# A mixture-of-experts layer: the second product on plain f32 operands instead of f32r high and low parts

## The chip, the core and the metric

The kernel runs on one core of a Trainium2 chip. The core has a matrix engine (TensorE, PE; its weight loads are shown apart as PEld), a vector engine (VectorE, DVE), an activation engine (ScalarE, ACT), a general engine (GpSimd, POOL) and a sync engine (SyncE, SP) that mostly issues transfers. The engines run their own programs and meet at semaphores. The metric is the device time of one execution in microseconds; lower is better.

## The reference, cut to what matters

Three stages follow each other on 32 sequences of 128 tokens with 128 features: the gradient of a soft sequence alignment, an attention with 8 heads, and a layer of 8 experts of which each token uses two. The change is in the last:

```python
def _L0_ffn_ref(x, Wg, W, V, W2):            # x: (32, 128, 128), layer-normed
    gate_logits = jnp.einsum('bsd,de->bse', x, Wg)
    topv, topi = jax.lax.top_k(gate_logits, K)          # K = 2 of E = 8
    w = jax.nn.softmax(topv, axis=-1)
    gw = jnp.sum(w[..., None] * jax.nn.one_hot(topi, E, dtype=x.dtype), axis=-2)
    y = jnp.zeros_like(x)
    for e in range(n_experts):                          # W, V: (8, 128, 512), W2: (8, 512, 128)
        h = jax.nn.silu(jnp.einsum('bsd,df->bsf', x, W[e])) * jnp.einsum('bsd,df->bsf', x, V[e])
        y = y + gw[..., e:e + 1] * jnp.einsum('bsf,fd->bsd', h, W2[e])
    return y
```

All of it is f32. `h @ W2[e]` is the second product.

## The kernel before

**Alignment** (0 to about 230 us) is a wavefront on DVE, ACT and POOL. **Attention** (about 230 to 590 us) works in 32 steps n, one block of 128 tokens each, with pieces that serve four blocks at once. The order on each engine is written out by hand: one Python loop over `STEPS_OF_ATTENTION` per engine, in which `pair` and `quad` place each piece some steps ahead or behind. Its last pieces sort every token's two copies by expert into the DRAM buffer `xd_dram` (POOL, L1038).

In the same steps the weights of the experts are brought in, in 24 chunks, chunk c in step c: SP loads 128x512 floats into one of two `stage` tiles (`load_weights`, L480 to L489), ACT copies them to an f32r tile as the high part (`weights_high`, L927 to L930), and DVE subtracts it from the f32 value for the low part (`weights_low`, L1405 to L1408). Chunks 0 to 15 are W and V, chunks 16 to 23 are W2, whose parts lie side by side in `wdn`.

**Experts** (about 590 to 820 us) works through 72 tiles of 128 token copies, all of one expert each. A product of two f32 matrices is done on f32r operands as high x high + high x low + low x high. For tile k:

- SP loads the rows (L517); PE turns them (`column`, L707); ACT copies the high part (`columns`, L953), DVE makes the low part (`column_low`, L1467).
- PE computes both first products, three matmuls of 512 columns each (`up`, L541 to L543, within the helper `three`).
- ACT applies silu (L959), DVE multiplies (`hidden`, L1453).
- PE turns the result in four pieces (`turn`, L727); ACT copies the high part to `xnt_hi` (`hidden_high`, L965), DVE makes the low part `xnt_lo` (`hidden_low`, L1474).
- PE computes the second product (`down`, L743 to L747): for each of four pieces, high part times both parts of `wdn` (256 columns, L743 and L747) and low part times the high one (128 columns, L744 and L746). Columns 0 to 127 of bank 6 then hold two of the three sums, columns 128 to 255 the third.
- ACT scales the third by the token's gate (`gated_low`, L973), DVE scales the others and adds it (`gated`, L1482), and POOL scatters the rows to `y_dram` (L1064).

The stages of different tiles are interleaved: on PE `up(k)`, `column(k + 1)`, `turn(k - 1)`, `down(k - 2)`. The expert of a tile is read from a table in `tili` by PE itself (`expert_of`, L756). PE's loop turns every eight tiles (`pe.Fori`, L780), DVE's and ACT's every four. `down(k)` waits for `s_y` of the tile before, since there is one bank 6; `up(k)` waits for `column_low(k)`.

At the end (820 to 844 us) SP loads the scattered rows, DVE adds them and SP stores the output.

Of the kernel before, what the change touches and what calls it, by code (L numbers as in the profile page):

```python
# [5 lines left out]
def tower(nc, tok_x, tok_y, we_t, w_proj, b_proj, w_gap, b_gap, iota66, wqk_pl, wv_bd, w_m, w_g, w_up, v_up, w_down,  # L6
# [27 lines left out]
    with ctx:  # L34
# [36 lines left out]
        nvt = sb("nvt", [128, NB])  # L71
        thf = sb("thf", [T, NB, T])
# [55 lines left out]
        ones_f = al("ones_f", [128, 128])  # L128
# [8 lines left out]
        zdiag = al("zdiag", [128, NB])  # L137
# [5 lines left out]
        wdn = sb("wdn", [128, NX, FC, 2, E], fr)  # L143

        def parts_of(c):

            kind, e = c // NX, c % NX
            staged = stage[c % 2][:]
            if kind == 2:
                return wdn[:, e, :, 0, :], wdn[:, e, :, 1, :], staged.rearrange("p (c n) -> p c n", n=E)  # L150
            hi, lo = ((wup_hi, wup_lo), (vup_hi, vup_lo))[kind]
            return hi[:, e, :], lo[:, e, :], staged
# [61 lines left out]
        hidt_hi, hidt_lo = xnt_hi, xnt_lo  # L214
        dest = sb("dest", [128, 4], i32)
        ylow = [on[1][:, k, :] for k in range(2)]
# [45 lines left out]
        s_wlo = sem("s_wlo")  # L262
        s_wraw = sem("s_wraw")
# [3 lines left out]
        s_htl = sem("s_htl")  # L267
# [55 lines left out]
        s_ylow = sem("s_ylow")  # L323
# [94 lines left out]
        CHUNKS = 3 * NX  # L418
# [3 lines left out]
        def _(sp):  # L422
# [57 lines left out]
            def load_weights(c):  # L480
# [4 lines left out]
                if kind < 2:  # L485
                    sp.dma_start(stage[c % 2][:], (w_up, v_up)[kind][e]).then_inc(s_stage[c % 2], 16)
                else:
                    sp.dma_start(stage[c % 2][:].rearrange("p (c n) -> p c n", n=E),
                                 w_down[e].rearrange("(c p) n -> p c n", p=128)).then_inc(s_stage[c % 2], 16)  # L489
# [48 lines left out]
        def _(pe):  # L538
# [181 lines left out]
            def turn(k, c):  # L720

                pe.wait_ge(s_hid, k + 1)
                if not (isinstance(k, int) and k < 2):
                    pe.wait_ge(s_ht, k - 1)
                    pe.wait_ge(s_htl, k - 1)
# [5 lines left out]
            def down(k, c, e):  # L731

                pe.wait_ge(s_ht, k + 1)
                pe.wait_ge(s_htl, k + 1)
                if not (isinstance(k, int) and k < 1):
                    pe.wait_ge(s_y, k)
                for n in range(FC):
                    b = slice(T * n, T * n + T)

                    low = [hidt_lo[c % 2][:, b], wdn[:, bass.ds(e, 1), n, 0, :].rearrange("p e n -> p (e n)")]  # L740
                    both = wdn[:, bass.ds(e, 1), n, :, :].rearrange("p e j n -> p (e j n)")
                    if n == 0:
                        nc.tensor.matmul(ps[:, 6, 0:2 * E], hidt_hi[c % 2][:, b], both, start=True, stop=False)  # L743
                        nc.tensor.matmul(ps[:, 6, 0:E], *low, start=False, stop=False)  # L744
                    else:
# [6 lines left out]
            pe.wait_ge(s_wlo, CHUNKS)  # L752
            pe.wait_ge(s_table, 1)
# [31 lines left out]
        def _(act):  # L785
# [175 lines left out]
            def hidden_high(k, c):  # L961
# [3 lines left out]
                nc.scalar.activation(hidt_hi[c % 2][:], ps[:, 5 + 2 * (c % 2), :], ACT.Copy).then_inc(s_ht, 1)  # L965

            def gated_low(k, c):

                act.wait_ge(s_dn, k + 1)
                act.wait_ge(s_dest, k + 1)  # L970
                if not (isinstance(k, int) and k < 2):
                    act.wait_ge(s_y, k - 1)
                nc.scalar.activation(ylow[c % 2], ps[:, 6, E:2 * E], ACT.Copy,  # L973
                                     scale=rowgate[:, c:c + 1]).then_inc(s_ylow, 1)

            def act_tile(k, c, head=False, tail=0):
# [4 lines left out]
                if not (head and k < 1) and tail < 3:  # L981
                    hidden_high(k - 1, (c + 3) % 4)
                if not (head and k < 2):
# [585 lines left out]
```

## Time and profile before

| | |
|---|---|
| median of 3 runs | 842.27 us (841.99 to 842.51) |
| profiled execution | 846.1 us |
| its span | 844.0 us |
| PE busy | 484.8 us (57%), weight loads 422.3 |
| DVE busy | 593.4 us (70%) |
| ACT busy | 406.8 us (48%) |
| POOL busy | 230.7 us (27%) |
| mean granted clock of PE | 0.983 |

The profile is one execution. Busy time is the time in which an engine's instructions run; matmuls overlap each other, so PE can read as busy while it could take more. A matmul's record covers its passage through the array, so the pace is read from the distance between starts, not from the durations. Shapes of f32r operands are printed without numbers or as f32.

### The profile page before, as it was taken

To read this page: it belongs to the slowest core of one execution; us is meant where nothing else is said; L and a number is where in the kernel's file an instruction comes from. 1 tells how busy PE (TensorE), PEld (TensorE's weight loads), DVE (VectorE), ACT (ScalarE), POOL (GpSimd) and SP (SyncE) were. 2 spreads that over 40 slices of the span, in tenths; PEclk is the share of its full clock that TensorE was granted. 3 is DMA by queue.
4 is the path that set the end of the run, shared out by engine and by line. 5 is a ranking of instruction groups with operands and counts; after the bars stand their busy time and mean duration, and the time that the engine had idled before them with its cause. 6 is when DMAs were issued, how large, how long until landed. Compare 5 with 4: busy or idle time off the path is not lost.

```text
span 844.0 us, 13480 instructions
## 1 busy us (share of the span) xinstructions
PE 484.8 (57%) x2622; PEld 422.3 (50%) x2623; DVE 593.4 (70%) x2029; ACT 406.8 (48%) x1180; POOL 230.7 (27%) x417
## 2 busy tenths in 40 slices
PE   1200000000004689899899998620899999999960
PEld 0200000000003578798788987610688888888850
DVE  3698989889747866978988674652466666666645
ACT  1344444444302867666666574100566656666630
POOL 1054545455300000000403312455133333333330
PEclk9999999999999999999999999999999999999985
DMA  4499230403254122222102000012111111111109
GB/s 98 90 177 165 45 72 10 82 1 81 41 137 125 51 75 63 63 75 62 52 26 67 26 7 20 26 38 64 35 45 42 44 43 44 41 43 43 44 16 287
DMA packets 113385, 54.18 MB, mean 64 GB/s; under 512 B 56652, under 2 KB 109132, under 8 KB 113251
## 3 DMA queue, kind: packets, MB, share of 16 engines
q1 hardware_dynamic: 106366, 44.60, 22.7%
q0 software_dynamic: 4352, 8.47, 3.0%
q10 hardware_dynamic: 2621, 0.62, 0.5%
q8 instruction: 14, 0.23, 0.1%
q14 instruction: 32, 0.26, 0.1%
HBM read 29.93 MB, written 24.26 MB: 64 GB/s over the span
## 4 chain that ended last, share of the span: by engine, by line
PE 36%; DVE 31%; issue 20%; DMA 5%; SPq 4%; ACT 3%; ACTq 0%; DVEq 0%; POOLq 0%
DVE D L1178 5%; PE ps L541 5%; DVE D L1153 5%; PE ps L543 5%; PE ps L542 5%; PE ps L747 4%; PE ps L627 4%; PE ps L727 4%; PE ps L632 3%; ACT D L819 2%; DVE D L1144 2%; PE ps L746 2%; PE ps L743 2%; DVE rc L1322 2%; DVE ps L1133 1%
## 5 line engine op out<-in xcount | busy, mean ns | idle before, releaser
L1038 POOL DMA_INDIRECT xd_dram<-pay,slot x64 | 64.8, 1013 | 281.3 <-DVE pay L1402 263.9
L632 PEld LDWEIGHTS ps<-va,pt 128*128 128x128 f32 x512 | 137.5, 351 | 0.0
L627 PE MATMUL ps<-eye_sb,sq 128*128 128x128 f32 x256 | 114.8, 454 | 13.9 <-DVE on L1339 10.3
L1064 POOL DMA_INDIRECT y_dram<-on,dest x72 | 70.7, 982 | 164.1 <-DVE on L1482 127.5
L632 PE MATMUL ps<-va,pt 128*128 128x17 f32 x512 | 114.7, 307 | 0.0
L577 PE MATMUL ps<-zdiag,ones_f 32*128 32x32 f32 x2 | 0.6, 406 | 193.0 <-DVE zdiag L1221 193.0
L627 PEld LDWEIGHTS ps<-eye_sb,sq 128*128 128x128 f32 x256 | 87.5, 343 | 34.4 <-issue 25.8
L577 PEld LDWEIGHTS ps<-zdiag,ones_f 32*128 32x128 f32 x2 | 0.5, 304 | 193.1 <-DVE zdiag L1221 193.1
L1022 POOL TENSOR_TENSOR D<-D 128x128 f32<-128x128 f32 x130 | 56.3, 433 | 129.3 <-DVE D L1171 65.0
L1453 DVE TENSOR_TENSOR sq<-sq,ps 128x512 f32<-128x512 f32 x72 | 49.5, 688 | 56.2 <-PE ps L543 41.1
L819 ACT ACTIVATE D<-D 64x2 f32<-64x2 f32 (+1 forms) x154 | 31.4, 204 | 106.9 <-DVE D L1153 86.9
L898 ACT ACTIVATE sq<-sq,mn 128x128 f32<-128x128 f32 x256 | 78.0, 395 | 0.0
L747 PE MATMUL ps<-wdn,xnt_hi 128*128 x216 | 57.8, 336 | 0.0
L959 ACT ACTIVATE sq<-ps 128x512 f32<-128x512 f32 x72 | 43.1, 598 | 27.1 <-PE ps L543 27.1
L891 ACT ACTIVATE sq<-ps 128x1024 f32<-128x1024 f32 x32 | 32.7, 1022 | 46.4 <-DVE mn L1324 42.2
L1178 DVE TENSOR_TENSOR_SCAN D<-ps,D 128x64 f32<-128x64 f32 x130 | 45.5, 350 | 13.5 <-ACT D L819 0.5
L1322 DVE TENSOR_REDUCE rc<-ps 128x8 f32<-128x1024 f32 x32 | 39.0, 1218 | 22.7 <-PE ps L607 11.9
L1474 DVE TENSOR_TENSOR xnt_lo<-ps,xnt_hi 128x512 fp32r<-128x512 f32 x72 | 49.8, 692 | 6.7 <-ACT xnt_hi L965 0.7
L746 PE MATMUL ps<-wdn,xnt_lo 128*128 x216 | 52.1, 241 | 0.0
L1153 DVE TENSOR_TENSOR_SCAN D<-ps,D 128x64 f32<-128x64 f32 x130 | 44.8, 345 | 6.9 <-DMA D<-th_dram 4.8
L965 ACT ACTIVATE xnt_hi<-ps 128x512 fp32r<-128x512 f32 x72 | 43.1, 598 | 7.6 <-PE ps L727 1.5
L607 PE MATMUL ps<-kx,qs 32*128 32x512 f32 x64 | 38.8, 705 | 11.0 <-ACT sq L891 7.5
(226 smaller groups left out, 1474.1 us busy)
## 6 DMA issues: line engine op xcount, KB each, us to landing
stage<-xd_dram SPq DMA_DIRECT2D x72, 65.0 KB, 1.8
D<-th_dram SPq DMA_DIRECT2D x16, 208.0 KB, 4.8
g_dram<-D SPq DMA_DIRECT2D x14, 208.0 KB, 4.6
x_dram<-D SPq DMA_DIRECT2D x14, 208.0 KB, 4.7
h0q<-g_dram SPq DMA_DIRECT2D x8, 256.0 KB, 3.0
gb<-g_dram SPq DMA_DIRECT2D x8, 256.0 KB, 3.5
xf<-x_dram SPq DMA_DIRECT2D x8, 256.0 KB, 3.2
xb<-x_dram SPq DMA_DIRECT2D x8, 256.0 KB, 3.5
```

Of the source, the lines that this page charges most:

```text
L627: last = nc.tensor.transpose(ps[:, 5 + h // 4, T * (h % 4):T * (h % 4) + T], sq[n % 3][:, T * h:T * h + T], eye_sb[:])
L632: m = nc.tensor.matmul(ps[:, 7, (HD + 1) * h:(HD + 1) * (h + 1)], pt[turned % 2][:, T * h:T * h + T], va[q % 2][:, k, h, :], start=True, s ...
L746: nc.tensor.matmul(ps[:, 6, 0:E], *low, start=False, stop=False)
L747: m = nc.tensor.matmul(ps[:, 6, 0:2 * E], hidt_hi[c % 2][:, b], both, start=False, stop=(n == FC - 1))
L898: m = nc.scalar.activation(v, v, ACT.Exp, bias=mn[:, n % 3, h:h + 1], scale=-1.0 / HD ** 0.5)
L1022: pool.tensor_tensor(C3[:, k, 0:2, :], shifted(M, at, 1, 2), bass.AP(tensor=n.tensor, offset=n.offset, ap=[n.ap[0], [H, 1], [0, 2], [1, H] ...
L1038: pool.indirect_dma_start(xd_dram, bass.IndirectOffsetOnAxis(slot[:, q, j, k:k + 1], 0), pay[q % 2][:, k, j, :], None).then_inc(s_sc[2 * k ...
L1064: pool.indirect_dma_start(y_dram, bass.IndirectOffsetOnAxis(dest[:, c:c + 1], 0), yrow[c], None, bounds_check=2 * NB * T - 1, oob_is_err=F ...
L1153: nc.vector.tensor_tensor_scan(row(M, at), above(k), TH[:, s, :], cells(M, at, 0, 1), ALU.max, ALU.subtract).then_inc(s_row, 1)
L1178: nc.vector.tensor_tensor_scan(row(X, at), weights_of(i * ROWS + k)[:, 2, :], V[:, k % 2, :], cells(X, at, 0, 1), ALU.mult, ALU.add).then_ ...
L1322: link(V_.tensor_reduce(rc[:, 0, :], ps[:, 3:5, :].rearrange("p a (h s) -> p (a h) s", s=T), AX.X, ALU.min, apply_absolute_value=True))
L1474: V_.tensor_tensor(hidt_lo[c % 2][:], ps[:, 5 + 2 * (c % 2), :], hidt_hi[c % 2][:].bitcast(f32), ALU.subtract).then_inc(s_htl, 1)
```

## The change

The weights W2 are loaded straight to their place, unsplit, in the same steps of the attention stage. The turned hidden tile is copied once, to new f32 tiles `hidt` (two, 128x512), and the second product is four f32 matmuls of 128 columns. `hidden_low` and `gated_low` are gone, and `gated` reads only bank 6. `zdiag` and `ones_f` move from the space that the alignment shares with later tiles to space of their own.

```diff
-        wdn = sb("wdn", [128, NX, FC, 2, E], fr)
+        wdn = sb("wdn", [128, NX, FC, E])
...
-        hidt_hi, hidt_lo = xnt_hi, xnt_lo
+        hidt = [sb(f"hidt{k}", [128, 512]) for k in range(2)]
...
-        CHUNKS = 3 * NX
+        CHUNKS = 2 * NX
...
+            def load_down(e):
+
+                sp.dma_start(wdn[:, e, :, :], w_down[e].rearrange("(c p) n -> p c n", p=128)).then_inc(s_wd, 16)
...
                 if 0 <= n + 3 < CHUNKS:
                     load_weights(n + 3)
+                if CHUNKS <= n < CHUNKS + NX:
+                    load_down(n - CHUNKS)
...
             def down(k, c, e):
 
                 pe.wait_ge(s_ht, k + 1)
-                pe.wait_ge(s_htl, k + 1)
                 if not (isinstance(k, int) and k < 1):
                     pe.wait_ge(s_y, k)
                 for n in range(FC):
-                    b = slice(T * n, T * n + T)
-
-                    low = [hidt_lo[c % 2][:, b], wdn[:, bass.ds(e, 1), n, 0, :].rearrange("p e n -> p (e n)")]
-                    both = wdn[:, bass.ds(e, 1), n, :, :].rearrange("p e j n -> p (e j n)")
-                    if n == 0:
-                        nc.tensor.matmul(ps[:, 6, 0:2 * E], hidt_hi[c % 2][:, b], both, start=True, stop=False)
-                        nc.tensor.matmul(ps[:, 6, 0:E], *low, start=False, stop=False)
-                    else:
-                        nc.tensor.matmul(ps[:, 6, 0:E], *low, start=False, stop=False)
-                        m = nc.tensor.matmul(ps[:, 6, 0:2 * E], hidt_hi[c % 2][:, b], both, start=False,
-                                             stop=(n == FC - 1))
+                    m = nc.tensor.matmul(ps[:, 6, 0:E], hidt[c % 2][:, T * n:T * n + T],
+                                         wdn[:, bass.ds(e, 1), n, :].rearrange("p e n -> p (e n)"),
+                                         start=(n == 0), stop=(n == FC - 1))
                 m.then_inc(s_dn, 1)
 
             pe.wait_ge(s_whi, CHUNKS)
             pe.wait_ge(s_wlo, CHUNKS)
+            pe.wait_ge(s_wd, 16 * NX)
...
-            def gated_low(k, c):
...
-                nc.scalar.activation(ylow[c % 2], ps[:, 6, E:2 * E], ACT.Copy,
-                                     scale=rowgate[:, c:c + 1]).then_inc(s_ylow, 1)
...
-            def hidden_low(k, c):
-                dve.wait_ge(s_ht, k + 1)
-                if not (isinstance(k, int) and k < 2):
-                    dve.wait_ge(s_dn, k - 1)
-                V_.tensor_tensor(hidt_lo[c % 2][:], ps[:, 5 + 2 * (c % 2), :], hidt_hi[c % 2][:].bitcast(f32),
-                                 ALU.subtract).then_inc(s_htl, 1)
...
             def gated(k, c):
 
-                dve.wait_ge(s_ylow, k + 1)
+                dve.wait_ge(s_dn, k + 1)
...
-                V_.scalar_tensor_tensor(yrow[c], ps[:, 6, 0:E], rowgate[:, c:c + 1], ylow[c % 2], ALU.mult,
-                                        ALU.add).then_inc(s_y, 1)
+                V_.tensor_scalar(yrow[c], ps[:, 6, 0:E], rowgate[:, c:c + 1], None, ALU.mult).then_inc(s_y, 1)
```

PE, inside the loop over the tiles, from the last turned pieces of one tile to its second product. Before (`sq` holds the hidden tile, `xnt_hi` and `xnt_lo` its turned parts; ISA rows compute an address from the expert's number):

```order
L727 MATMUL ps<-eye_sb,sq 128x128 x3
L756 ISA
L756 TENSOR_LOAD tili
L756 ISA x2
L743 ISA [waits s_y,s_htl,s_ht]
L743 MATMUL ps<-wdn,xnt_hi 128x256
L744 MATMUL ps<-wdn,xnt_lo 128x128
L746 ISA
L746 MATMUL ps<-wdn,xnt_lo 128x128
L747 MATMUL ps<-wdn,xnt_hi 128x256
```

PE at the same place now (L724 is the turning, L745 the table, L734 the second product):

```order
L724 MATMUL ps<-eye_sb,sq 128x128 x3
L745 ISA
L745 TENSOR_LOAD tili
L745 ISA x2
L734 ISA [waits s_y,s_ht]
L734 MATMUL ps<-wdn,hidt 128x128
L734 ISA
L734 MATMUL ps<-wdn,hidt 128x128
```

The product keeps its place behind the turning and the table read, and keeps its wait for `s_y`; the wait for the low part is gone.

DVE, one tile inside its loop, before:

```order
L1453 TENSOR_TENSOR sq<-sq,ps 128x512 [waits s_htp,s_up]
L1464 REGISTER_ALU
L1466 ISA [waits s_xc]
L1467 TENSOR_TENSOR ont_lo<-ps,ont_hi 128x128 [waits s_up]
L1460 COPY rowgate<-stage 128x1 [waits s_ys3,s_xr3]
L1461 CAST dest<-stage 128x1
L1474 TENSOR_TENSOR xnt_lo<-ps,xnt_hi 128x512 [waits s_dn,s_ht]
L1482 SCALAR_TENSOR_TENSOR on<-ps,rowgate,on 128x128 [waits s_ys1,s_ylow]
```

DVE now (L1431 was L1453, L1445 was L1467, L1453 was L1482):

```order
L1431 TENSOR_TENSOR sq<-sq,ps 128x512 [waits s_htp,s_up]
L1442 REGISTER_ALU
L1444 ISA [waits s_xc]
L1445 TENSOR_TENSOR ont_lo<-ps,ont_hi 128x128 [waits s_up]
L1438 COPY rowgate<-stage 128x1 [waits s_ys2,s_xr2]
L1439 CAST dest<-stage 128x1
L1453 TENSOR_SCALAR on<-ps,rowgate 128x128 [waits s_ys0,s_dn]
```

The subtraction is gone, and the last operation waits for PE (`s_dn`) where it waited for ACT (`s_ylow`).

## Rows read from the trace of the kernel before

**Rows 1.** The page, 40 slices of the span: PE busy tenths and granted clock.
```profile
PE   1200000000004689899899998620899999999960
...
PEclk9999999999999999999999999999999999999985
```

**Rows 2.** Stretches: from:to, length, busy us (count) by engine, clock, DMA share, GB/s.
```profile
400.00:475.00 75.00, 70.40 (x330) 62.34 (x330) 61.83 (x220) 48.06 (x125) 19.19 (x18) 1.00 0.15 46
...
700.00:800.00 100.00, 97.73 (x629) 84.97 (x628) 67.70 (x199) 60.75 (x132) 32.41 (x33) 1.00 0.16 43
```

**Rows 3.** Groups, 600 to 800 us: line, shapes, count | busy, mean ns | idle before.
```profile
L747 PE MATMUL ps<-wdn,xnt_hi 128*128 x198 | 52.4, 333 | 0.0
...
L1474 DVE TENSOR_TENSOR xnt_lo<-ps,xnt_hi 128x512 fp32r<-128x512 f32 x67 | 46.3, 692 | 5.9 <-ACT xnt_hi L965 0.2
...
L973 ACT ACTIVATE on<-ps,rowgate 128x128 f32<-128x128 f32 x65 | 23.9, 367 | 31.5 <-PE ps L747 30.2 <-DVE dest L1461 1.3
```

**Rows 4.** One tile on PE in time order: start us, us, engine, line, operation.
```profile
623.98 0.42 PE L541 MATMUL ps<-wup_hi,ont_hi 128*128 x1
...
625.50 0.60 PE L727 MATMUL ps<-eye_sb,sq 128*128 128x128 f32 x4
...
626.87 0.40 PE L541 MATMUL ps<-wup_hi,ont_hi 128*128 x1
```

**Rows 5.** All engines in time order at the loop's turn.
```profile
626.70 0.33 PE L747 MATMUL ps<-wdn,xnt_hi 128*128 x1
...
627.54 0.35 DVE L1482 SCALAR_TENSOR_TENSOR on<-ps,rowgate,on 128x128 f32<-128x128 f32 x1
...
628.80 0.19 PEld L744 LDWEIGHTS ps<-wdn,xnt_lo 128*128 128x128 f32 x1
...
629.16 0.28 DVE L1467 TENSOR_TENSOR ont_lo<-ps,ont_hi 128x128 fp32r<-128x128 f32 x1
...
629.49 0.19 PEld L747 LDWEIGHTS ps<-wdn,xnt_hi 128*128 128x128 f32 x1
...
630.14 0.19 PEld L541 LDWEIGHTS ps<-wup_hi,ont_hi 128*128 128x128 f32 x1 [0.46 <-issue]
...
632.77 0.19 PEld L743 LDWEIGHTS ps<-wdn,xnt_hi 128*128 128x128 f32 x1 [0.62 <-issue]
```

**Rows 6.** PE in time order, the first tile of the experts.
```profile
593.50 0.63 PE L542 MATMUL ps<-wup_lo,ont_hi 128*128 x1
593.93 0.63 PE L543 MATMUL ps<-wup_hi,ont_lo 128*128 x1
```

**Rows 7.** Plain f32 products in time order.
```profile
34.23 0.50 PEld L571 LDWEIGHTS ps<-raw_m,raw_v 128*128 128x128 f32 x2 [9.24 <-DVE cnt L1109]
34.23 0.80 PE L571 MATMUL ps<-raw_m,raw_v 128*128 128x128 f32 x2 [8.97 <-DVE cnt L1109]
...
34.95 0.58 PE L572 MATMUL ps<-uv,cnt 22*128 22x1 f32 x2
...
412.78 1.85 PE L673 MATMUL ps<-wg_sb,x3t 128*128 128x8 f32 x8 [2.38 <-issue]
```

**Rows 8.** The last tile's second product in time order.
```profile
814.88 0.58 PE L743 MATMUL ps<-wdn,xnt_hi 128*128 x1 [1.04 <-DVE on L1482]
...
815.58 0.52 PE L747 MATMUL ps<-wdn,xnt_hi 128*128 x1
...
816.43 0.52 PE L747 MATMUL ps<-wdn,xnt_hi 128*128 x1
```

**Rows 9.** Instructions on wdn (ns min/median/max, from, to), then PE's waits, 400 to 475 us.
```profile
L1408 DVE TENSOR_TENSOR wdn<-stage,wdn x8: 679/682/685, 415.2 to 472.4; 128x512 fp32r<-128x512 f32 x8
...
PE ps L673 <- issue: 3.7, 2, 2.4
```

**Rows 10.** DVE and PE in time order, one step of the attention stage.
```profile
442.53 0.68 DVE L1408 TENSOR_TENSOR wdn<-stage,wdn 128x512 fp32r<-128x512 f32 x1
...
446.81 0.57 PE L673 MATMUL ps<-wg_sb,x3t 128*128 128x8 f32 x2 [1.28 <-issue]
```

More of the change, by code:

```diff
@@ L71, in tower @@
         nvt = sb("nvt", [128, NB])
+        zdiag = sb("zdiag", [128, NB])
+        ones_f = sb("ones_f", [128, 128])
         thf = sb("thf", [T, NB, T])
@@ L213, in tower @@
         hid = [sq[1][:, F * k:F * k + F] for k in range(2)]
-        hidt_hi, hidt_lo = xnt_hi, xnt_lo
+        hidt = [sb(f"hidt{k}", [128, 512]) for k in range(2)]
         dest = sb("dest", [128, 4], i32)
-        ylow = [on[1][:, k, :] for k in range(2)]
         rowgate = sb("rowgate", [128, 4])
@@ L262, in tower @@
         s_wlo = sem("s_wlo")
+        s_wd = sem("s_wd")
         s_wraw = sem("s_wraw")
@@ L484, in load_weights @@
                 need(sp, s_wlo, c - 1)
-                if kind < 2:
-                    sp.dma_start(stage[c % 2][:], (w_up, v_up)[kind][e]).then_inc(s_stage[c % 2], 16)
-                else:
-                    sp.dma_start(stage[c % 2][:].rearrange("p (c n) -> p c n", n=E),
-                                 w_down[e].rearrange("(c p) n -> p c n", p=128)).then_inc(s_stage[c % 2], 16)
+                sp.dma_start(stage[c % 2][:], (w_up, v_up)[kind][e]).then_inc(s_stage[c % 2], 16)
+            def load_down(e):
+                sp.dma_start(wdn[:, e, :, :], w_down[e].rearrange("(c p) n -> p c n", p=128)).then_inc(s_wd, 16)
             for n in STEPS_OF_ATTENTION:
@@ L959, in silu, with hidden_turned @@
                 nc.scalar.activation(act_up[c % 2], ps[:, 1 + c % 2, :], ACT.Silu).then_inc(s_silu, 1)
[L961 removed]
+            def hidden_turned(k, c):
                 act.wait_ge(s_htp, k + 1)
@@ L964, in hidden_high @@
                     act.wait_ge(s_dn, k - 1)
-                nc.scalar.activation(hidt_hi[c % 2][:], ps[:, 5 + 2 * (c % 2), :], ACT.Copy).then_inc(s_ht, 1)
-            def gated_low(k, c):
-                act.wait_ge(s_dn, k + 1)
-                act.wait_ge(s_dest, k + 1)
-                if not (isinstance(k, int) and k < 2):
-                    act.wait_ge(s_y, k - 1)
-                nc.scalar.activation(ylow[c % 2], ps[:, 6, E:2 * E], ACT.Copy,
-                                     scale=rowgate[:, c:c + 1]).then_inc(s_ylow, 1)
+                nc.scalar.activation(hidt[c % 2][:], ps[:, 5 + 2 * (c % 2), :], ACT.Copy).then_inc(s_ht, 1)
             def act_tile(k, c, head=False, tail=0):
@@ L981, in act_tile @@
                 if not (head and k < 1) and tail < 3:
-                    hidden_high(k - 1, (c + 3) % 4)
-                if not (head and k < 2):
-                    gated_low(k - 2, (c + 2) % 4)
+                    hidden_turned(k - 1, (c + 3) % 4)
             columns(0, 0)
@@ L991, in _ @@
                     act_tile(t + c, c)
-            for k in range(TILES - 4, TILES + 2):
+            for k in range(TILES - 4, TILES + 1):
                 act_tile(k, k % 4, tail=max(0, k - TILES + 2))
@@ L1491, in dve_tile @@
                     destination(k, c)
-                if not (head and k < 1) and tail < 3:
-                    hidden_low(k - 1, (c + 3) % 4)
                 if not (head and k < 2):
```

9 lines of the change are left out of this document (removed).

## The prediction

> **What bounds the kernel now.** I read the page first: PE is full from slice 14 on, in the attention stage and then, from about 590 us, in the experts [rows 1]. The change touches the experts, and the conversion of their weights, which sits in the attention stage. The stretches come next [rows 2]: between 700 and 800 us PE is busy for 97.7 of 100 us, DVE for 67.7 and ACT for 60.8. So PE sets the pace of a tile, and work taken from DVE or ACT there gives nothing by itself. In the groups L747 runs 198 times in 200 us, three per tile, hence 66 tiles of 3.03 us [rows 3].
>
> Then I read one tile in order of time [rows 4]. From L541 at 623.98 to the next tile's L541 at 626.87 are 2.89 us: six products of 512 columns and a turned tile up to 625.50, then four turned pieces of 128 f32 columns, (0.60 - 0.27)/3 = 0.11 apart (0.60 is the group, 0.27 the passage of one), and the second product. With 0.11 for the turned tile the six are (625.50 - 623.98 - 0.11)/6 = 0.235 apart. What limits the second product's eight matmuls is their weight loads, not their columns: from the second load (628.80) to the eighth (629.49) are six steps in 0.69 us, 0.115 each [rows 5], with matmuls of 128 and 256 columns behind them in turn.
>
> The difference between 3.03 and 2.89 is time in which PE has nothing issued: at the loop's turn, which comes every eight tiles, the first load of L541 (630.14) has 0.46 us of "issue" before it, and the first load of L743 after it (632.77) has 0.62 [rows 5].
>
> PE's clock: the six products of the very first tile are 0.43 apart (593.50 to 593.93) [rows 6], later ones 0.235 [rows 4]. These are the two levels, 1.2 and 2.4 GHz. The page's clock line reads 9 in the attention stage too [rows 1], but L673 there has eight loads (1.85 - 0.36)/7 = 0.21 apart [rows 7], and 0.21 is also the pace of loads in the last tile, (816.43 - 815.58)/4, where the page's line shows the lower level [rows 1, 8]. I go by the spacings: attention ran at 1.2 GHz.
>
> **Part 1: the second product on PE.** Four plain f32 matmuls of 128 columns per tile take the place of eight f32r ones. The trace records every plain f32 product twice: L571 is one matmul in the code and has two loads and two matmuls, L673 is four and has eight [rows 7]; turned f32 pieces are recorded once, four for four [rows 4]. So there are again eight passes per tile, each with a weight load of 128 f32 columns. What one pass costs is the disputed number; the trace has no f32 product of 128 columns at the higher clock. Its loads: L673's take 0.21 at 1.2 GHz as the f32r ones do [rows 7, 8], so at 2.4 GHz they cost the same 0.115. Its columns: L571 is the one case, at 1.2 GHz (it runs at 34 us, among PE's first work). Its second load starts at 34.23 + 0.50 - 0.34 = 34.39 (0.34 is one load's passage) and its second matmul at 34.23 + 0.80 - 0.42 = 34.61: the first pass of columns took at most 0.22, or 0.11 at 2.4 GHz. The second ended before L572 begins at 34.95, at most 0.34, or 0.17 [rows 7]. Four turned pieces of 128 f32 columns go 0.11 apart at the higher clock [rows 4]. So the ends for a pass are 0.11 and 0.17, and I take 0.115, the value next to the turned pieces: load and columns run beside each other, and the load is the longer by a hair. 8 x 0.115 = 0.92 per tile before and after: **0 us**. At 0.17 it would be 0.055 x 8 x 72 = +32 us. At the other end little is to be had: L541 also waits for DVE's L1467, which ends at 629.44, while PE would load for L541 at 629.49 + 0.115 = 629.60 if it did not pause there [rows 5]. Of these 0.16 PE's own steps between the wait and the load take most, so I give it 0.06 per tile to come forward: 0.06 x 72 = -4 us is the bound.
>
> A rule of the Trainium skill speaks against this change: "FP8 and Floating Point Precision", section "TensorE Precision Notes", says that true FP32 takes four passes through the array. By that rule the second product streams 4 x 4 x 128 = 2048 columns per tile instead of 4 x 128 + 4 x 256 = 1536, an estimated third more of column time, and becomes slower. The two recorded matmuls per f32 product [rows 7], each with its columns at half speed, agree with the four passes; whether they cost anything is what the loads decide.
>
> **Part 2: DVE and ACT in the experts.** Gone per tile are L1474 (0.69 us, DVE) and L973 (0.37, ACT) [rows 3]; L1482 (0.35) becomes a one-source product, nearest row L1467 with 0.28 [rows 5]. PE covers all of it. What comes earlier is the release of y: today L747 ends at 626.70 + 0.33 = 627.03, L1482 starts 0.51 later (0.37 of it L973) and ends at 627.89 [rows 5]. PE's program waits for that y before it issues the second product and turns the loop, and L541's load comes 2.25 us later (630.14), after PE has run dry. Without L973, and with 0.28 for 0.35, y comes 0.44 earlier. I credit 0.3 of it, since the waits in front of it in PE's program (for the turned pieces) take part of that time anyway; the ends are 0 and the whole 0.46. The turn back is taken seven times: 7 x 0.3 = **-2.1 us** (0 to -3.2). The 0.62 before L743 follows table reads of PE's own; it stays.
>
> **Part 3: the last tiles.** Here nothing hides behind PE: L743 at 814.88 had waited 1.04 us for L1482 [rows 8]. The second product of a tile waits for the y of the tile before, since they share one bank. Without L973 (0.37) and with the shorter DVE operation each such link is 0.44 shorter. There are three: before the last two products and before the last scatter, 3 x 0.44 = 1.3 us. The very last product ran at the lower clock: its loads took 8 x 0.21 = 1.7 us instead of 0.9 [rows 8]. If it comes earlier and denser it may stay at 2.4 GHz. I take half of those 0.9: **-1.75 us** (-1.3 to -2.2).
>
> **Part 4: the weights in the attention stage.** Eight loads go straight to their place; eight DVE subtractions (0.68, 415.2 to 472.4) [rows 9] and as many ACT copies are gone. PE is busy there for 70.4 of 75 us [rows 2], so only its pauses count: 3.7 us in two pauses before L673 [rows 9]. The longer, 2.38 ahead of 412.78 [rows 7], precedes the first removed subtraction and stays. The shorter, 1.28 ahead of 446.81, hangs on work on DVE that starts directly behind L1408 at 442.53 (the reduction of L1322, then queries and keys, L1312 to L1316) [rows 10]; without L1408 it starts up to 0.68 earlier. With a part of the smaller pauses: **-1.0 us** (0 to -2.5; all of PE's idle time there is 4.6). The experts begin behind a scatter and a table that follow PE's work, so I let it carry through. On SP the eight transfers no longer wait for DVE; behind them in the queue are the loads of the next batch, which can only come earlier.
>
> **Sum.** 0 - 2.1 - 1.75 - 1.0 = -4.85 us. The profiled execution took 846.1 us (span 844.0 and 2.1 around it), so it would be 841.25. The median of the runs shown is 842.27, 3.8 less than the profiled execution; with the same difference the median becomes **837.4 us**.
>
> **Rivals.**
> - *The columns decide.* Eight passes of f32 columns at 0.11 [rows 4] are 0.88 us per tile; today's 1536 columns, at 0.235 per 512 [rows 4], are 0.70. If the loads do not hide the columns but add to them, the tile grows by 0.18, x 72 = +13: 842.27 - 4.85 + 13 = 850.4. For it speaks the thin margin between 0.115 and 0.11. Against it, today's loads at an even 0.115 whatever stands behind them [rows 5]. It decides from a pass of 0.115 + 4.85/576 = 0.123 us on. Chance 0.13, and 0.03 for a pass near 0.17, about 869. (By the page's four passes this case would be the likeliest.)
> - *The clock falls.* In the attention stage PE was full with f32 work [rows 1], and its spacings were those of 1.2 GHz. If plain f32 in a third of each tile brings that back, a tile takes 6 x 0.43 + 5 x 0.21 + 8 x 0.21 = 5.3 us instead of 2.9: +170 us. Against it: the first products are untouched, and after six of them the clock was up [rows 6, 4]. Chance 0.04.
> - *Nothing but the tail.* The loop's turn is held by PE's own reads and branch, and the pause at 446 opens again one step later. 842.27 - 1.3 = 841.0. Chance 0.15.
> - *The second product gets shorter*, to the limit of DVE's L1467: another -4, 833.4. Chance 0.08.
>
> **How the numbers follow.** The forecast has 0.57; its own range is 834.5 to 840. A measurement of this kernel can tell about 0.2% (1.7 us) from no change. Faster: 0.54 of the forecast, 0.08, and 0.03 of the third rival, 0.65. Same: 0.03 and 0.12, 0.15. Slower: 0.20. The range that should hold 8 in 10 leaves out the clock and the upper half of the column rival: 832 to 850.
>
> **What would show it.** In the trace after: eight loads per tile for the second product 0.115 apart and tiles of 2.86 to 2.89 us (Part 1; 0.13 or more means the first rival); the "issue" time before L541's first load at the loop's turn down from 0.46 to under 0.2, with y some 0.45 earlier (Part 2); under 0.7 us waited before the last product instead of 1.04 (Part 3); no idle over 0.8 near 445 us (Part 4). First products 0.43 apart after 600 us would be the clock.

## The result, and the profile after

The changed kernel took 835.55 us (median of 4 runs, 835.21 to 836.18), the kernel before 842.38 (841.99 to 842.51) on the same chip: ratio 0.9921, 95% interval 0.9903 to 0.9938. Forecast were 837.4 us (834.5 to 840 for the likeliest case alone) and a gain of 4.85; it came to 6.8. On another chip (run a1 below) the ratio was 0.9947 (0.9931 to 0.9964), 835.94 against 840.74 us. By the two ratios the gain is thus 4.5 to 6.7 us.

In the changed kernel the second product is L734, the six products L539 to L541, the turned tile L705, the turned pieces L724, y L1453, the hidden pieces' copy L954, the product with `w_g` L671.

The page of the kernel after, PE's busy tenths and its clock (to be held against [rows 1]):

```profile
PE   1200000000004589899899999630799999999960
...
PEclk9999999999999855555555555555799999999995
```

The clock line now shows the lower level in the attention stage, where before's page read 9. The forecast had taken 1.2 GHz there from spacings alone, and PE's product with `w_g` takes the same 1.85 us as in [rows 7]. So the clock line can read 9 in a stage that ran at 1.2 GHz (a second profile of the changed kernel, a1, again shows 9 there), and the spacings decide.

The stretches of the kernel after (same columns as [rows 2]):

```profile
400.00:475.00 75.00, 71.64 (x337) 63.62 (x337) 58.55 (x215) 45.47 (x117) 19.99 (x19) 0.50 0.09 27
700.00:800.00 100.00, 99.26 (x642) 86.47 (x641) 45.74 (x167) 49.46 (x101) 33.15 (x34) 1.00 0.16 42
```

DVE gave up 22 of its 67.7 us per 100 and ACT 11, and PE, which sets the pace, filled from 97.7 to 99.3. In the groups of 600 to 800 us the new operations read (line, shapes, count | busy, mean ns | idle before):

```profile
L734 PE MATMUL ps<-wdn,hidt 128*128 x538 | 72.8, 278 | 2.0 <-issue 2.0
...
L1453 DVE TENSOR_SCALAR on<-ps,rowgate 128x128 f32<-128x128 f32 x67 | 23.5, 351 | 28.6 <-PE ps L734 28.6
```

538 matmuls for 67 tiles are eight per tile: the program has four, and each is recorded twice, as the prediction read from [rows 7]. L1453, with one source fewer, takes 351 ns, as L1482 did (0.35, [rows 5]); the forecast had given it 0.28.

PE's loads, PE and DVE in time order at the loop's turn (its first tile starts at 624.84), against [rows 5]:

```profile
623.68 0.97 PEld L734 LDWEIGHTS ps<-wdn,hidt 128*128 128x128 f32 x8
...
624.84 0.19 PEld L539 LDWEIGHTS ps<-wup_hi,ont_hi 128*128 128x128 f32 x1 [0.18 <-issue]
...
624.88 0.35 DVE L1453 TENSOR_SCALAR on<-ps,rowgate 128x128 f32<-128x128 f32 x1 [0.33 <-PE ps L734]
...
627.29 0.97 PEld L734 LDWEIGHTS ps<-wdn,hidt 128*128 128x128 f32 x8 [0.51 <-issue]
```

Eight loads in 0.97 us with 0.19 for the last are (0.97 - 0.19)/7 = 0.111 apart. The pause at the turn fell from 0.46 to 0.18, the next one, before the second product, from 0.62 to 0.51.

The last two second products and the last y in time order, against [rows 8]:

```profile
804.23 1.13 PE L734 MATMUL ps<-wdn,hidt 128*128 x8 [0.19 <-DVE on L1453]
...
805.98 1.13 PE L734 MATMUL ps<-wdn,hidt 128*128 x8 [0.62 <-DVE on L1453]
...
807.15 0.35 DVE L1453 TENSOR_SCALAR on<-ps,rowgate 128x128 f32<-128x128 f32 x1 [1.40 <-PE ps L734]
```

The wait before the last product is 0.62 instead of 1.04. Its eight matmuls pass in 1.13 us: it ran at the higher clock, where before's ran at the lower.

What holds an ordinary tile, away from the turn, is not the second product alone. DVE's low part of the turned column, and the first load of the next tile's products, before and after:

```profile
626.29 0.28 DVE L1467 TENSOR_TENSOR ont_lo<-ps,ont_hi 128x128 fp32r<-128x128 f32 x1
...
626.77 0.19 PEld L541 LDWEIGHTS ps<-wup_hi,ont_hi 128*128 128x128 f32 x1
```

```profile
615.53 0.28 DVE L1445 TENSOR_TENSOR ont_lo<-ps,ont_hi 128x128 fp32r<-128x128 f32 x1
...
616.01 0.19 PEld L539 LDWEIGHTS ps<-wup_hi,ont_hi 128*128 128x128 f32 x1
```

In both the load starts 0.20 us after DVE's operation ends (626.57 and 615.81). The same 0.20 stands in five of every eight tiles of the loop, in both kernels. Behind the last load of the second product it comes 0.13 to 0.14 later in the kernel before (0.24 in one tile of the eight) and 0.16 now (0.27 in one), where the product's own loads follow each other by 0.115 and 0.111. So the tile stays at 2.87 us although the product's loads have moved a little closer together. That this wait sets the tile is read from the traces; no run moved L1445 by itself.

### The profile page after: what moved, and what is told of

Same layout as the page of the kernel before. It is cut to its first block, busy times and chain, and to the rows that moved or that the text cites. A ratio compares the mean times of both kernels' runs of the same rounds, so it can differ in the third digit from the quotient of the medians.

```text
span 833.7 us, 13145 instructions
## 1 busy us (share of the span) xinstructions
PE 484.2 (58%) x2622; PEld 421.8 (51%) x2623; DVE 539.5 (65%) x1949; ACT 377.2 (45%) x1100; POOL 230.2 (28%) x417
## 3 DMA queue, kind: packets, MB, share of 16 engines
HBM read 29.93 MB, written 24.26 MB: 65 GB/s over the span
## 4 chain that ended last, share of the span: by engine, by line
PE 46%; DVE 30%; issue 8%; DMA 6%; ACT 3%; SPq 3%; POOL 3%; ACTq 0%; DVEq 0%; POOLq 0%
PE ps L734 8%; PE ps L625 7%; PE ps L539 6%; DVE D L1156 5%; PE ps L630 5%; DVE D L1131 5%; PE ps L541 5%; PE ps L540 5%; PE ps L724 4%; POOL xd_dram L1016 3%; PE ps L605 3%; ACT D L808 2%; DVE D L1122 2%; DVE ps L1111 2%; DMA xd_dram<-pay,slot 1%
## 5 line engine op out<-in xcount | busy, mean ns | idle before, releaser
L1431 DVE TENSOR_TENSOR sq<-sq,ps 128x512 f32<-128x512 f32 x72 | 49.5, 687 | 90.4 <-PE ps L541 67.7
L734 PE MATMUL ps<-wdn,hidt 128*128 x576 | 77.9, 278 | 2.9 <-issue 2.0
L734 PEld LDWEIGHTS ps<-wdn,hidt 128*128 128x128 f32 x576 | 69.9, 192 | 7.1 <-issue 7.1
L954 ACT ACTIVATE hidt<-ps 128x512 f32<-128x512 f32 x72 | 43.0, 597 | 8.6 <-PE ps L724 2.6
L1453 DVE TENSOR_SCALAR on<-ps,rowgate 128x128 f32<-128x128 f32 x72 | 25.3, 351 | 32.6 <-PE ps L734 32.6
```

The costliest lines, as they stand in the source:

```text
L734: m = nc.tensor.matmul(ps[:, 6, 0:E], hidt[c % 2][:, T * n:T * n + T], wdn[:, bass.ds(e, 1), n, :].rearrange("p e n -> p (e n)"), start=(n ...
L1431: V_.tensor_tensor(hid[c % 2], act_up[c % 2], ps[:, 3 + c % 2, :], ALU.mult).then_inc(s_hid, 1)
```

## The experiments

A ratio is always to the kernel before on the same chip. Its median there was 842.38 us for the changed kernel's first runs, 841.38 for e1 to e4, 840.74 for a1, e5, e8 and e7, 847.36 for b1, e9 and e10, and 846.84 for e11. So medians of different groups are not compared, and a difference of 1 us between two ratios lies within their intervals. Since a few tenths matter, I read lengths from each profile, measured between starts of PE's first product of a tile (L539 in the changed kernel): "eight tiles" is the mean length of a pass through PE's loop of eight tiles, "tail" the time from the last tile's first product to the last scatter. "Last send" is the start of the last scatter of the attention stage.

| kernel | median us | ratio (95%) | last send at | eight tiles | tail |
|---|---|---|---|---|---|
| before, the profile of [rows 1 to 10] | 842.27 | | 583.78 | 24.26 | 9.82 |
| b1, before again | 843.7, one run | | 582.08 | 24.28 | 8.96 |
| after | 835.55 | 0.9921 (0.9903-0.9938) | 580.13 | 23.88 | 7.66 |
| a1, after again | 835.94 | 0.9947 (0.9931-0.9964) | 580.02 | 23.88 | 7.68 |
| e1, weights back | 837.73 | 0.9966 (0.9952-0.9980) | 581.74 | 24.04 | 7.68 |
| e2, y through ACT | 838.10 | 0.9962 (0.9948-0.9976) | 579.61 | 24.04 | 8.88 |
| e3, low part back | 837.62 | 0.9957 (0.9942-0.9971) | 580.28 | 24.07 | 8.01 |
| e4, all three back | 840.45 | 0.9989 (0.9980-0.9999) | 580.44 | 24.12 | 8.88 |
| e5, half the columns | 835.12 | 0.9930 (0.9914-0.9947) | 580.20 | 23.88 | 7.51 |
| e8, twice the columns | 885.27 | 1.0527 (1.0509-1.0544) | 579.71 | 29.33 | 10.45 |
| e7, loop of 32 | 836.13 | 0.9947 (0.9930-0.9963) | 580.04 | see there | 7.68 |
| e9, loop of 16 | 839.28 | 0.9907 (0.9883-0.9931) | 584.02 | 23.53 | 7.67 |
| e10, copies only | 842.35 | 0.9936 (0.9911-0.9962) | 581.51 | 23.88 | 7.68 |
| e11, two waits | 842.60 | 0.9938 (0.9916-0.9959) | 582.82 | 23.98 | 7.68 |

**First group: each part undone in the changed kernel.** e1 brings the weights' way through the stage back, with ACT's copies and DVE's subtractions:

```diff
-        CHUNKS = 2 * NX
+        CHUNKS = 3 * NX
...
+                    sp.dma_start(stage[c % 2][:].rearrange("p (c n) -> p c n", n=E),
+                                 w_down[e].rearrange("(c p) n -> p c n", p=128)).then_inc(s_stage[c % 2], 16)
...
-                if CHUNKS <= n < CHUNKS + NX:
-                    load_down(n - CHUNKS)
...
-                V_.tensor_tensor(lo, staged, hi.bitcast(f32), ALU.subtract).then_inc(s_wlo, 1)
+                V_.tensor_tensor(lo, staged, hi if c >= 2 * NX else hi.bitcast(f32), ALU.subtract).then_inc(s_wlo, 1)
```

> The changed kernel with the eight W2 chunks brought in as before: through the stage tiles, with an ACT copy (into the f32 tile wdn) and a DVE subtraction (into a spare tile) each. Theory: the first experts' product came 6.1 us earlier in the changed kernel's profile, and 3.35 us of that (at the last block's scatter: 0.3 before the first removed operation, 3.65 behind the last) are the removed operations; so the median rises by about 3.3 us over 835.55, to 838.9, and the growth lies between 400 and 530 us. Rival: that gain is an accident of two single executions (the one of before was 3.8 us above its median); then the median stays at 835.5 to 836.5.

PE in time order around 445 us (start, length, engine, line), first after, then e1:

```profile
445.33 1.85 PE L671 MATMUL ps<-wg_sb,x3t 128*128 128x8 f32 x8 [0.68 <-issue]
```

```profile
423.08 0.45 PE L630 MATMUL ps<-eye_sb,sq 128*128 128x128 f32 x1 [0.63 <-DVE on L1321]
...
447.05 1.20 PE L676 MATMUL ps<-wg_sb,x3t 128*128 128x8 f32 x5 [1.28 <-issue]
```

Held against after step by step, e1 is 0.50 us late up to 421 us, 1.12 from 429 on, 1.72 from 447 on, and stays so to the last send (1.6): two steps, 0.62 and 0.60. The second is the pause that the prediction named [rows 10], 1.28 with the subtraction and 0.68 without; the first is a wait of PE for DVE that it had only as "a part of the smaller pauses". So the weights are worth 1.22 us. Every kernel that has the subtractions shows the same two steps at the same two places, together 1.21 to 1.22 us: both profiles of the kernel before, e1 and e4 below. None of the others has them. The expected 3.3 us did not come from the weights; the larger steps that the first profile of the kernel before has at 484 and 514 us are of another kind (see e10).

One thing is not explained: in e1 the fifth of the eight tiles takes 3.10 instead of 2.98 in every turn, 1.0 us in all. Its PE program has one wait fewer ahead of the tiles, but so have e4 and e10, which keep 2.98.

e2 puts an ACT operation between the product and DVE's y, as before:

```diff
+                nc.scalar.activation(ylow[c % 2], ps[:, 6, 0:E], ACT.Copy,
+                                     scale=rowgate[:, c:c + 1]).then_inc(s_ylow, 1)
...
-                V_.tensor_scalar(yrow[c], ps[:, 6, 0:E], rowgate[:, c:c + 1], None, ALU.mult).then_inc(s_y, 1)
+                V_.scalar_tensor_tensor(yrow[c], ps[:, 6, 0:E], rowgate[:, c:c + 1], ylow[c % 2], ALU.mult, ALU.max).then_inc(s_y, 1)
```

> The changed kernel with an ACT operation of 0.37 us put back between the second product and the DVE operation that writes y (DVE takes the larger of the two equal values, so y is the same but comes later). Theory: an early y shortens the turn of PE's loop (0.19 us on each of seven tiles, part of 0.24 on each of eight) and each link in the last tiles (0.41, three of them, and 0.8 if the last product falls to the lower clock). So +2.5 to +3.8 us, 838.0 to 839.4, with the period of the loop's last tile back near 3.19. Rival: the turn is held by PE's own program; then only the tail shows, +1.2, 836.8, and the loop's last tile stays at 3.00.

e2's loads at the turn and its last second product:

```profile
624.78 0.19 PEld L541 LDWEIGHTS ps<-wup_hi,ont_hi 128*128 128x128 f32 x1 [0.38 <-issue]
...
807.88 1.13 PE L736 MATMUL ps<-wdn,hidt 128*128 x8 [1.02 <-DVE on L1466]
```

The turn's pause is 0.38 again instead of 0.18, the last tile of the eight takes 3.17 instead of 3.00, and the wait before the last product is back at 1.02. Of the 0.4 us by which y comes earlier, PE gets 0.17 per turn, and the tail all of it, three times: 8.88 - 7.66 = 1.22. That is the theory of the expectation, and not its rival.

e3 brings back DVE's subtraction of the hidden pieces and PE's two waits for it, with nothing using the result:

```diff
+                    pe.wait_ge(s_htl, k - 1)
...
+                pe.wait_ge(s_htl, k + 1)
...
+                V_.tensor_tensor(xnt_lo[c % 2][:], ps[:, 5 + 2 * (c % 2), :], hidt[c % 2][:],
+                                 ALU.subtract).then_inc(s_htl, 1)
```

> The changed kernel with the DVE subtraction of 0.69 us per tile put back (into a tile that nothing reads) and PE's two waits for it. Theory: DVE's time is free, but PE's program has one wait instruction more before the turned pieces of the loop's first tile, where PE is starved by its own program: 0.1 us on each of eight tiles, and some of the early y lost. So +0.8 to +1.5 us, 836.4 to 837.1; normal tiles stay at 2.87. Rival: DVE's 0.69 us per tile were worth something in every tile (the chain over the low part of the columns is only 0.06 off the path); then +0.06 x 72 = +4, 839.9, and normal tiles grow to 2.93.

e3 at the turn:

```profile
624.08 0.97 PEld L737 LDWEIGHTS ps<-wdn,hidt 128*128 128x128 f32 x8
...
625.02 0.69 DVE L1455 TENSOR_TENSOR xnt_lo<-ps,hidt 128x512 fp32r<-128x512 f32 x1
...
625.36 0.19 PEld L540 LDWEIGHTS ps<-wup_hi,ont_hi 128*128 128x128 f32 x1 [0.31 <-issue]
625.62 0.34 DVE L1463 TENSOR_SCALAR on<-ps,rowgate 128x128 f32<-128x128 f32 x1
```

The subtraction lies across the place of y: y starts 1.54 after the product's first load (624.08 to 625.62), in the changed kernel 1.20 (623.68 to 624.88). Tiles away from the turn stay at 2.87 us, though DVE is busy for 66.0 instead of 45.7 us per 100: PE covers it there. At the turn the last tile grows by 0.10 and the next by 0.12, 0.19 with what the following one gives back. The tail grows too, from 7.66 to 8.01: with ACT's link gone, DVE's subtraction stands ahead of y there as well.

e4 has all three back; it is the kernel before but for the product itself.

> All three put back: this is the kernel before but for the second product itself, four f32 matmuls (eight passes) instead of eight f32r ones. Theory: the passes cost the same on PE (steps of 0.112 after, 0.115 before), so nearly the whole gain goes: 842.38 less 0.02 x 72 = 841 to 842.4. Rival: part of the gain is the f32 product's own, by fewer address computations or less traffic; then it stays under 840.

The product alone gives 0.9989 (0.9980 to 0.9999), about 0.9 us. Its eight tiles take 24.12 against 24.27 of the kernel before, nearly all of it in the two tiles at the turn (3.48 for 3.59, 3.16 for 3.20; by the starts of the loads 3.46 for 3.48 and 3.16 for 3.27, so only the sum is firm). The median lies between what the theory (841 to 842.4) and the rival (under 840) gave. Its tail is 8.88, no longer than e2's: with ACT's link in place the subtraction costs nothing there.

**Second group: what a pass costs.** a1 is the changed kernel again.

> The changed kernel unchanged, on the same chip as the next three, for the lengths of its stretches. Both theories: ratio to before 0.992 +- 0.002, so about 835 us; last send of the attention stage at 579.5 to 581, 5.3 to 5.5 us from it to the first tile, last tiles' stretch 7.7 us. If the clock's rise among the first tiles is a matter of chance, the second tile takes 2.9 us in one profile and 4.1 in another.

Its stretches agree with those of the first profile to about 0.1 us, as both theories had it; the ratio, 0.9947, is above the expected 0.992 +- 0.002, and that difference between chips stays open.

```diff
 e5: four products of 64 columns
-                    m = nc.tensor.matmul(ps[:, 6, 0:E], hidt[c % 2][:, T * n:T * n + T],
+                    h = 64 * (n // 2)
+                    m = nc.tensor.matmul(ps[:, 6, h:h + 64], hidt[c % 2][:, T * n:T * n + T],
+                                         wdn[:, bass.ds(e, 1), n, h:h + 64].rearrange("p e n -> p (e n)"),
...
 e8: four products of 256 columns
+                    f = min(n, FC - 2)
+                    m = nc.tensor.matmul(ps[:, 6, 0:2 * E], hidt[c % 2][:, T * n:T * n + T],
+                                         wdn[:, bass.ds(e, 1), f:f + 2, :].rearrange("p e j n -> p (e j n)"),
```

> Each plain f32 matmul of the second product streams 64 columns instead of 128 (it leaves out half of that product: pieces 0 and 1 give columns 0 to 63, pieces 2 and 3 columns 64 to 127); the eight weight loads per tile stay. Theory 'the loads set the pace of the second product': loads stay 0.110 to 0.112 apart, tiles stay 2.87 us, the time is that of the changed kernel within 1.5 us (834 to 837). Theory 'the columns set it': passes shrink toward half, up to 8 x 0.05 = 0.4 us per tile off PE, of which L541's wait for the turned pieces lets at most some 0.1 through, so 0 to -7 us, spacing of loads well under 0.11.

> Each plain f32 matmul of the second product streams 256 columns instead of 128 (128 of them are another piece's weights, their sum goes to unused columns of the bank; the output is unchanged); weight loads unchanged. Pass = two per matmul, eight per tile. If a pass is the longer of load (0.11) and columns (0.11 per 128 columns at half speed, hence 0.21 per 256), loads are 0.21 apart and each tile grows by 8 x 0.10 = 0.8 us: +58 us, about 893. If columns of plain f32 ran at the speed of f32r (0.235/512 = 0.00046 us each, 0.117 per 256) the spacing would stay near 0.117 and the time near +3 us, 838 to 840.

In one point e8's expectation is wrong: its last piece is multiplied by the third piece's weights, so the output is not unchanged. The work per matmul is as stated. The second product's loads in one tile, e5, then e8:

```profile
614.96 0.97 PEld L734 LDWEIGHTS ps<-wdn,hidt 128*128 128x128 f32 x8
```

```profile
615.14 0.97 PEld L735 LDWEIGHTS ps<-wdn,hidt 128*128 128x128 f32 x8
```

```profile
611.92 1.49 PEld L735 LDWEIGHTS ps<-wdn,hidt 128*128 128x128 f32 x7
...
615.48 1.60 PEld L735 LDWEIGHTS ps<-wdn,hidt 128*128 128x128 f32 x8
```

(The first of the three is the changed kernel's; in the row of seven the first load is not recorded.) With 64 columns the loads are 0.111 apart as with 128, and nothing is gained. With 256 the second load follows the first by 0.11 (1.60 - 1.49), and the others are (1.49 - 0.19)/6 = 0.217 apart; a plain tile grows from 2.87 to 3.67 us. So the pass takes the longer of the load, 0.111, and its columns, 0.217/256 = 0.00085 us each. For 128 columns that is an estimated 0.108, if their time is in proportion to their number; no run measured it, since at 128 the loads hide it. That the tile of e5 stays at 2.87 says less than its spacing does: its next tile's first load is held 0.20 us behind DVE's low part like the changed kernel's. The +58 us expected came to +49.3 because the longer product hides the turn's pauses (all tiles of e8's loop take 3.66 to 3.67).

e7 lets PE's loop turn every 32 tiles:

```diff
-            with pe.Fori(4, TILES - 4, 8) as t:
-                pe_tiles(t, 8)
+            with pe.Fori(4, TILES - 4, 32) as t:
+                pe_tiles(t, 32)
```

(The table that PE reads is 24 entries longer for it.)

> PE's loop over the tiles turns every 32 tiles instead of every 8 (more table entries read per turn, none changed): 1 turn inside the stage instead of 7 between its blocks, so 6 of the turn's pauses go. Theory 'each turn costs PE its branch and the reads after it': in the changed kernel the turn's tile and the one after are 0.13 and 0.48 us above the plain 2.87 us tile. If all of that goes: 6 x 0.6 = -3.7 us, 831.5. If the pause after the turn is made by reads of the table that come with any eight tiles, only the 0.13 goes: -0.8 us, 834.5.

No gain. Away from its one turn, eight tiles take 23.18 us (six of 2.87 and two of 2.98), so a turn costs the changed kernel 23.88 - 23.18 = 0.70. Six turns less are -4.2 us. But the one turn that is left is long. PE there in time order:

```profile
696.59 0.79 PE L539 MATMUL ps<-wup_hi,ont_hi 128*128 x1 [3.27 <-issue]
697.18 0.63 PE L540 MATMUL ps<-wup_lo,ont_hi 128*128 x1
697.60 0.63 PE L541 MATMUL ps<-wup_hi,ont_lo 128*128 x1
```

and its stretch (columns as [rows 2]):

```profile
696.00:703.00 7.00, 6.41 (x22) 5.60 (x23) 1.47 (x5) 1.47 (x3) 0.00 (x0) 0.52 0.07 21
```

PE stands for 3.27 us with nothing issued, and from the end of this pause on it has the clock of 0.5 for 6.8 us: the three tiles there take 6.36, 5.35 and 3.23 us, 5.5 more than around a turn of the changed kernel. With 1.3 us gained at the second tile (below) that makes the same 213.8 us. The queue that loads instructions moved 28 packets in this kernel and 14 in the changed one, two of them between 690 and 697 us (packets, MB, share):

```profile
q8 instruction: 2, 0.03, 1.9%
```

In the changed kernel this queue moves nothing from 626 to 800 us, and in e9, with 16 tiles per turn, nothing from 643 to 795; in e7 it moves six packets of 16 KB between 710 and 800 alone. That the longer loop's code had to be fetched again at the turn, and the shorter ones' not, fits this, and it is read from the traces, not tested.

**Third group, on a chip where the kernel before took 847 us.** e9 turns every 16 tiles.

> PE's loop turns every 16 tiles: four blocks instead of eight. A turn costs 0.81 us in the changed kernel (its eight tiles take 23.88 us, eight tiles inside the loop of 32 took 23.07), four of them go: -3.2 us against the changed kernel, if the clock stays up as it does there. The loop of 32 lost all of its 5 us to a stretch of 6.8 us at the granted clock 0.5 after 105.8 us without a pause. If that stretch follows any longer run without a pause, it appears here too and costs 6.3 us: then +3 us or more instead of -3.

No low stretch and no long pause. The 64 tiles of the loop take 188.2 us against 191.0: four turns less at 0.70 are 2.8 (the 0.81 and 23.07 in the expectation were summed wrongly). Its ratio, 0.9907 (0.9883 to 0.9931), is the lowest measured, but its interval overlaps those of the changed kernel; what shows the gain of 2.8 us is the profile. The theory that a longer run without a pause brings the low clock has fallen: 16 tiles without one did no harm, and in e7 the low clock came right after a pause.

> The kernel before, unchanged, in a new profile: its profiled execution was 3.8 us above its median, and all kernels run since have 5.3 to 5.6 us between the attention stage's last send and the experts' first tile where it had 7.8. If those were that one execution's, this profile has the last send at 581 to 582 us, 5.3 to 5.6 us behind it, a span near 840 and the same stretch of the experts (215.8). If they belong to the kernel, 583.8 and 7.8 come back.

The tail and the eight tiles are what belongs to the kernel. The span was 841.6 us and the experts' stretch 217.2, longer than the expected 215.8 by its second tile (4.12 us for 2.85). The last send came at 582.08, and the gap from it to the first turned tile of the experts was 6.4 us, between the 7.8 of the first profile and the 5.3 to 5.7 of all others in the first two groups: it belongs to the execution. SyncE's eight padding writes make it, in time order in the changed kernel, in b1 and in e10:

```profile
568.26 8.40 SPq L500 DMA_DIRECT2D xd_dram<-padt  x8
```

```profile
570.85 13.15 SPq L502 DMA_DIRECT2D xd_dram<-padt  x8
```

```profile
570.72 15.74 SPq L505 DMA_DIRECT2D xd_dram<-padt  x8
```

They are about 1.1 us apart in the changed kernel's execution and about 2.1 in e10's, and where they end after the last send (580 to 584 us) the experts wait for them.

e10 is e1 without DVE's part (n counts the chunks that DVE subtracts; the waits are cut to match):

```diff
-                if 0 <= n < CHUNKS:
+                if 0 <= n < 2 * NX:
```

> Of the weights' old way only ACT's eight copies through the stage come back to the changed kernel, not DVE's eight subtractions. With both, the attention stage ended 1.6 us later (581.74 against 580.02 and 580.13). Theory of the prediction (DVE's 0.68 us each are what counts): within 0.4 us of the changed kernel, last send at 580.0 to 580.4. Rival (the stage, its transfers and ACT's place count): the 1 to 1.6 us come back without DVE's part, 836.5 to 837.5.

In e10 neither of e1's two steps is there: against after it is 0.35 us late at 421, 429, 447 and 454 us alike, and the pause that was 1.28 is 0.68:

```profile
445.69 1.85 PE L676 MATMUL ps<-wg_sb,x3t 128*128 128x8 f32 x8 [0.68 <-issue]
```

Later steps, at 461 and 484 us, are also in e9 and e11, whose weights come straight, so they are not the copies'; a last one at 514 us is in these three too. They made its last send 581.51 where 580.0 to 580.4 was expected. The subtractions are the cost, the copies and the stage are none.

e11 repeats two waits that have just been met:

```diff
                    pe.wait_ge(s_ht, k - 1)
+                    pe.wait_ge(s_ht, k - 1)
...
                pe.wait_ge(s_ht, k + 1)
+                pe.wait_ge(s_ht, k + 1)
```

> The changed kernel with two more wait instructions per tile in PE's program, each a repeat of a wait that has just been met (one before the turned pieces, one before the second product), so they hold nothing up by themselves. Bringing back DVE's subtraction with PE's two waits on it had cost 0.19 us per turn of the loop (positions 0 and 7 of the eight tiles +0.12 and +0.10, position 1 -0.05). Theory 'PE's own instructions at the turn cost it': eight tiles of the loop take 24.0 to 24.1 us instead of 23.88, +1 to +1.5 us in all. Rival 'it was DVE's operation that came late': 23.88 as in the changed kernel, time within 0.5 us of it.

Eight tiles take 23.98 us, 0.10 more: the tile after the turn 3.48 instead of 3.35, the next 3.03 instead of 3.08, the last of the eight 3.00 as before. So of e3's 0.19 the part behind the turn is PE's own wait instructions, and the part ahead of it (0.10) is left for DVE's subtraction. The median says nothing on this, since the changed kernel did not run on that chip.

## Why the prediction was right

**Part 1, the product on PE, 0 us.** Right in its reason. The loads are 0.111 apart, tiles away from the turn 2.87 us, before and after (2.89 by [rows 4]), and the runs with 64 and 256 columns show the maximum of load and columns. The margin, 0.111 against an estimated 0.108 for the columns, was as thin as the forecast had it. In ordinary tiles there was a second one that it did not use: the next tile's first load waits for DVE's low part, and lies 0.13 to 0.16 behind the last load of the product, 0.11 of which is the load's own time. For the same reason the bound of -4 us was too wide: the 0.06 per tile was worked out at the turn's tile, but in ordinary tiles the load already stood at its limit.

The trace agrees with the four passes of which the Trainium skill speaks ("FP8 and Floating Point Precision", section "TensorE Precision Notes") in so far as each of the two recorded passes streams at 0.00085 us per column, about half the speed of the f32r products (0.235/512 = 0.00046, [rows 4]). By these spacings eight passes of 0.108 against 1536 columns at 0.00046, 0.87 us against 0.70 a tile, are an estimated quarter more column time, where the rule gave a third, and the loads hid it. What the part missed is a small gain at the turn (e4, about 1 us).

**Part 2, the loop's turn, -2.1 us; measured -3.2.** The mis-sized term. (24.28 - 23.88) x 8 = 3.2, or 2.8 for the seven turns the prediction counts. In two points it gave y too much: DVE's operation was not shorter (0.351, so y comes 0.4 earlier and not 0.44), and of that only 0.17 per turn reaches PE (e2), not 0.3. The step that failed to the other side is "the 0.62 ... stays". It fell to 0.51: PE's program has fewer waits (0.10 per turn, e11). And two effects were not in the sum at all: DVE's subtraction no longer stands ahead of y (0.10, e3), and the product itself gives 0.15 (e4). These do not simply add: 0.17 + 0.10 + 0.10 + 0.15 = 0.52 against 0.40 in all. Why four f32 matmuls gain at the turn over eight f32r ones was not tested further; PE's program being shorter by four instructions per tile would do it.

**Part 3, the tail, -1.75; measured -1.3 or -2.2.** The three links gave 8.96 - 7.66 = 1.30, the 3 x 0.44 of the forecast, and this was in part luck: the 0.07 per link for a shorter DVE operation did not come. ACT's link is 1.22 of it (e2), but only because DVE's subtraction, which the part did not mention, went too; alone it would have kept 0.35 (e3). The other 0.08 is the product's own (e4, 8.88 for 8.96). The clock term was half taken: against the profile of [rows 8], where the last product ran low, it is another 9.82 - 8.96 = 0.86, against b1 nothing. Whether the clock falls before the last product is not the change's doing alone.

**Part 4, the weights, -1.0; measured -1.22** (e1, e10), 0.60 at the place named and 0.62 at one not named.

**Sum.** -3.2 - 1.3 - 1.2 = -5.7, and -6.6 with the last product's clock. The two comparisons give -6.7 (0.9921) and -4.5 (0.9947), on either side; the remainder is within what the attention stage and its padding writes vary by. That the forecast's 4.85 lies between the two is partly luck: the turn gave 1.1 more than its term, the weights 0.2 more, and the clock term of 0.45 measured 0.86 in one comparison of profiles and nothing in the other.

**The rivals.** "The columns decide" is out: the loads are no further apart with 128 columns than with 64 (e5), and if columns were added to the loads they would be 0.22 apart. With 256 columns they do decide, and cost 49 us (e8). The clock did not fall, with plain f32 in a third of each tile; the price set for it was right, since the tile that e7 ran wholly at the lower clock took 5.35 us. "Nothing but the tail" is out by e1 and e2. "The product gets shorter" is out by the changed kernel itself: its loads came 0.111 instead of 0.115 apart, and the ordinary tile did not shrink, held by L1445. Whether a product with fewer loads would gain once L1445 came earlier was not tested.

## What to carry to other kernels

A matmul pass with its own weight load costs the longer of load and columns; here 128 columns of plain f32 just fit behind a load, so plain f32 replaced a high and low split at no cost on PE, and with 256 columns it would have lost. Before you shorten such a product, look at what the next load waits for: here it stood 0.20 us behind an operation of DVE in most tiles, and a shorter product would have gained nothing. Count what the split's helpers cost at the places where PE stands still, the turn of its loop, the tail and each stage's reductions, and not by their busy time, which PE covered. When an engine's program sets a pause, its waits and reads count as instructions too, but a longer loop body can bring a new pause at its turn: 16 tiles were better than 8, 32 were not.

## What the runs showed of the hardware that was not expected

- Two waits that were already met cost PE 0.10 us per turn of the loop (e11), but nothing in tiles where it runs ahead.
- PE's clock rises within the first tile or the second, by the execution: the second tile takes 2.85 or 4.12 us, with the same kernel before (2.85 in one profile, 4.12 in b1). That is 1.3 us, more than most terms here.
- After a pause of 3.27 us among full work PE had the lower clock for 6.8 us (e7).
- The instruction queue was silent while PE's loops of 8 and 16 tiles turned, and moved a packet of 16 KB about every 13 us while the loop of 32 did (e7).
- The eight padding writes on one queue took 8.4 us in one execution and 15.7 in another, and the experts begin 5.3 to 9.8 us after the last send accordingly.
